# Attention and top-2 mixture of experts on one Trainium2 core: batch 1 routed in halves, scatters and weight parts placed anew, the last batch routed at the first tiles

## Chip, cores and metric

One core of one Trainium2 chip. The metric is the device time of one execution in microseconds (us), the median of the runs; lower is better.

## What is computed

```python
x = L0_attn_x                                   # (4, 1024, 128)
h = layernorm(x)
s = einsum('nsd,ntd->nst', h * w_lhs, h * w_rhs)
x = x + einsum('nst,ntd->nsd', softmax(s), h)
h2 = layernorm(x).reshape(4096, 128)
p = softmax(h2 @ router_w.T)                    # 8 experts, the best two kept and renormalised
y = sum over the two: gate * (gelu(h2 @ w_fc[e] + b_fc[e]) @ w_proj[e] + b_proj[e])
out = x + y
```

## The kernel before, in words

The program is written out by hand for each engine; an engine runs its list in order, and semaphores (`wait_ge`, `then_inc`) tie the lists together. There are two halves: attention over four batches, then the experts in tiles.

**Attention.** A batch b (0 to 3) has 1024 tokens, eight token tiles of 128, in two halves ("units" u = 2b and 2b+1). In stage b TensorE (PE) computes 16 blocks of scores (`score`, L1075 to L1077, three matmuls each, since the operands are split into a high and a low part). VectorE (DVE) takes the maximum of each block (`row_max`, L1409), `join_max` (L1419 to L1425) collects eight of them, PE turns them (`turn_negs`, L1084), ScalarE (ACT) keeps them (`keep_rows`), PE adds them to the scores (`shift_scores`, L1088), ACT takes the exponentials (`exponent`, L922) and PE multiplies with the values (`attend`, L1099, four matmuls a block, eight blocks a half). `add_attention` (L1433 to L1440) divides by the sums and adds to the residual `res`; the last exponentials of a batch wait for `shift_again` (L1414). At the boundary between stages PE also computes the router's sums (`route`, L1111 and L1112), which `keep_hrw` (L1368) reads.

**Routing.** In stage b+1 the logits of batch b are complete (`add_logits`); `take_stats2` and `take_moments2` on DVE and `scale_ln2` on GpSimd (POOL; a power, L740) give the second layernorm, ACT writes the normalised rows (`make_h2`, `high_h2`) and `split_h2` (L1472) their low part. `picks` (12 small DVE instructions) finds the two experts of a token, `rank_round` on PE with `keep_ranks` and `find_slots` on DVE the row of a slot table in DRAM, `gate_powers` on POOL (L783) the gate. Then POOL scatters the rows, 16 indirect DMAs a batch (`dispatch`, L774). A routing "round" is a batch or a half of one: `ROUNDS` lists them, and before the change only batch 2 is in halves. The scatters are paced in POOL's list by waits for a given maximum or exponential (`PACE_OWN`, `PACE_MAX`, `PACE_NEXT`).

**Weights.** ACT scales the eight 128x512 pieces of `w_fc` and POOL subtracts to get their low part (`low_part`, L748): three in the first part of stage 1, two in its second, then `clear_empty` and `store_empty` (L754 to L764) write filler rows into the slot table, which must have landed before the first scatter; the last three come in stage 3.

**Tiles.** 39 tiles of 256 rows, each of one expert. `make_table` (28 small DVE instructions, last L534) says for a group of tiles which expert each has and from which row it is loaded; there are three groups: tiles 0 to 7, 8 to 15, the rest. SyncE (SP) loads a tile (`slots_in`) once the group's table is made and its batches are scattered: batches 0 and 1 for the first group, batch 2 for the second, batch 3 for the third. Step k on PE turns tile k+2 (`turn_slots`, L1269), multiplies tile k up (L1281 to L1283) and tile k-2 down (L1302). ACT does gelu, and in its first steps the second layernorm of batch 3. DVE does `keep_rows` (L1731 to L1739), the bias (`add_bias`, L1746) and the gate (L1753) of tile k-3, and among the first steps the routing of batch 3 and the second table. POOL returns each tile with two indirect DMAs (L873). At the end SP loads all results, DVE adds them and SP stores.

## Time and profile before

| | |
|---|---|
| median of 3 runs | 331.57 us (331.29 to 331.64) |
| the profiled execution | 331.83 us, of which the span is 330.1 us |
| mean granted clock of TensorE | 0.948 of full |
| PE busy | 280.7 us, 85% |
| DVE busy | 225.1 us, 68% |
| ACT busy | 192.6 us, 58% |
| POOL busy | 185.5 us, 56% |
| chain that ended last | PE 59%, DVE 21%, DMA 6%, issue 5%, POOL 4% |

The span counts from the first to the last instruction of the profile; all positions below are us from its start. Stage 1 runs from about 46 to 83, stage 2 to 121, stage 3 to 165, the tiles to 299, and the rest is the way out. A busy share says little here, since each stage has its own limit; idle time of PE and what ended it says more.

### The profile page before, as it was taken

The page shows a single profiled execution, that of the slowest core. Times are in us where ns is not written, and L with a number is a line of the kernel's source. Part 1 is how long each engine was busy: PE and PEld are TensorE (multiplying, and loading weights), DVE is VectorE, ACT ScalarE, POOL GpSimd, SP SyncE. Part 2 cuts the span into 40 slices and gives each one's busy share as a digit, 9 for nine tenths or more (in the row PEclk, how much of TensorE's full clock was granted, in tenths as well). Part 3 has the DMA queues.
Part 4 walks back from the last instruction along what each step waited for, and adds up shares of the span by engine and source line. Part 5 has one row for each costly group of instructions (what it writes and reads, how often), then busy time and mean ns, then how long its engine had stood idle before and what let it go on. Part 6 is the DMA issues. An engine that isn't in the chain of part 4 may idle for free.

```text
span 330.1 us, 7870 instructions
## 1 busy us (share of the span) xinstructions
PE 280.7 (85%) x2197; PEld 250.0 (76%) x2198; DVE 225.1 (68%) x894; ACT 192.6 (58%) x388; POOL 185.5 (56%) x247
## 2 busy tenths in 40 slices
PE   8999998989979995995979999899999999994000
PEld 3588995878858894784968999799999999993000
DVE  4898879898867789799689778345444545453065
ACT  3455567957195634754389877567676767670000
POOL 8030035380777526768778777777777755567200
PEclk9999999999999999799899999999999999998555
DMA  6940000030011100101511531343333321111398
GB/s 204 426 203 0 0 3 0 3 118 13 18 42 43 34 14 29 50 26 42 156 45 44 131 109 52 93 135 101 99 91 88 91 81 47 50 42 48 116 354 317
DMA packets 16948, 29.37 MB, mean 89 GB/s; under 512 B 3760, under 2 KB 12848, under 8 KB 16656
## 3 DMA queue, kind: packets, MB, share of 16 engines
q1 hardware_dynamic: 12080, 18.40, 17.5%
q0 software_dynamic: 4832, 10.53, 9.6%
q8 instruction: 17, 0.28, 0.4%
q14 instruction: 19, 0.16, 0.2%
HBM read 16.30 MB, written 12.62 MB: 88 GB/s over the span
## 4 chain that ended last, share of the span: by engine, by line
PE 59%; DVE 21%; DMA 6%; issue 5%; POOL 4%; ACT 2%; SPq 1%; POOLq 0%; DVEq 0%; ACTq 0%
PE av_ps L1302 17%; PE av_ps L1099 14%; DVE neg_piece L1409 6%; PE sc_ps L1281 4%; PE sc_ps L1282 4%; PE sc_ps L1283 4%; DMA raw_proj<-results 4%; PE bank L1269 2%; PE bank L1088 2%; PE sc_ps L1088 1%; PE bank L1075 1%; DVE tile_start L534 1%; PE bank L1077 1%; PE bank L1076 1%; PE sc_ps L1076 1%
## 5 line engine op out<-in xcount | busy, mean ns | idle before, releaser
L873 POOL DMA_INDIRECT results<-prob,result_row x78 | 74.8, 959 | 32.0 <-issue 12.8
L774 POOL DMA_INDIRECT slots<-stage,slot x64 | 63.6, 993 | 39.1 <-DVE stage L1569 18.8
L1099 PE MATMUL av_ps<-h_all,prob 128*128 128x137 f32 x512 | 73.9, 289 | 3.6 <-DVE lg_part L1440 3.6
L1016 ACT ACTIVATE raw_fc<-sc_ps,bfc,scale_down 128x256 f32<-128x256 f32 x156 | 75.1, 570 | 2.1 <-PE sc_ps L1283 2.1
L1302 PE MATMUL av_ps<-raw_proj,raw_fc 128*128 x624 | 75.8, 275 | 0.0
L1099 PEld LDWEIGHTS av_ps<-h_all,prob 128*128 128x128 f32 x512 | 68.1, 194 | 7.4 <-DVE res L1437 5.1
L1302 PEld LDWEIGHTS av_ps<-raw_proj,raw_fc 128*128 128x128 f32 x624 | 72.6, 192 | 0.5
L1746 DVE TENSOR_TENSOR h_all<-av_ps,bpr 128x256 f32<-128x256 f32 x39 | 16.5, 424 | 48.9 <-PE sc_ps L1283 46.5
L1281 PE MATMUL sc_ps<-h_all,wfc_hi 128*128 128x256 f16 x156 | 42.6, 273 | 1.3 <-ACT raw_fc L1016 1.1
L1008 ACT ACTIVATE h_all<-bank 128x512 f16<-128x512 f16 x39 | 23.2, 596 | 34.5 <-PE sc_ps L1283 30.7
L1282 PE MATMUL sc_ps<-h_all,wfc_hi 128*128 128x256 f16 x156 | 42.5, 273 | 0.0
L1283 PE MATMUL sc_ps<-h_all,wfc_lo 128*128 128x256 f16 x156 | 42.5, 273 | 0.0
L1409 DVE TENSOR_REDUCE neg_piece<-bank 128x1 f32<-128x512 f32 x32 | 21.9, 684 | 8.3 <-PE bank L1077 4.2
L922 ACT ACTIVATE prob<-sc_ps 128x512 f32<-128x512 f32 x32 | 18.4, 599 | 11.4 <-PE sc_ps L1088 11.4
L912 ACT ACTIVATE again<-bank 128x512 f32<-128x512 f32 x16 | 9.5, 593 | 23.5 <-DVE neg_piece L1409 23.5
L1409 DVE TENSOR_REDUCE neg_piece<-sc_ps 128x1 f32<-128x512 f32 x32 | 21.8, 683 | 0.8 <-PE sc_ps L1077 0.7
L1753 DVE TENSOR_SCALAR prob<-h_all,row_gate 128x128 f32<-128x128 f32 x78 | 20.7, 338 | 1.4
L1281 PEld LDWEIGHTS sc_ps<-h_all,wfc_hi 128*128 x156 | 15.2, 98 | 3.6 <-issue 1.8
L932 ACT ACTIVATE h<-res,shift,rstd 128x128 f32<-128x128 f32 x32 | 14.7, 490 | 4.0 <-POOL shift L743 3.3
L1269 PE MATMUL bank<-ident,slots_in 128*128 128x128 f16 x156 | 14.9, 219 | 2.0 <-DMA slots_in<-slots 1.3
L1283 PEld LDWEIGHTS sc_ps<-h_all,wfc_lo 128*128 x156 | 15.3, 98 | 1.8
L1075 PE MATMUL bank<-hT_hi,q_hi 128*128 128x512 f32 x32 | 14.9, 465 | 2.0 <-ACT again L912 1.7
(183 smaller groups left out, 508.4 us busy)
## 6 DMA issues: line engine op xcount, KB each, us to landing
slots_in<-slots SPq DMA_DIRECT2D x39, 132.0 KB, 2.2
raw_fc<-in_w_fc_dram SPq DMA_DIRECT2D x1, 2048.0 KB, 10.9
raw_proj<-in_w_proj_dram SPq DMA_DIRECT2D x1, 2048.0 KB, 15.2
raw_fc<-results SPq DMA_DIRECT2D x2, 1024.0 KB, 7.4
raw_proj<-results SPq DMA_DIRECT2D x2, 1024.0 KB, 12.0
out_dram<-res SPq DMA_DIRECT2D x4, 512.0 KB, 5.0
res<-in_x_dram SPq DMA_DIRECT2D x3, 512.0 KB, 5.8
results<-prob,result_row POOLq DMA_INDIRECT x78, 2.3
```

The lines of the kernel that those rows point to most:

```text
L774: pool.indirect_dma_start(out=slots[:, :], out_offset=bass.IndirectOffsetOnAxis(ap=slot[:, n, k:k + 1], axis=0), in_=stage[:, b % 2, t, :] ...
L873: pool.indirect_dma_start(out=results[:, :], out_offset=bass.IndirectOffsetOnAxis(ap=result_row[a][:, h:h + 1], axis=0), in_=gated[a][h], ...
L1008: act.activation(xT[:, a % NH, :], bank[a % 2][:, :].bitcast(F16)[:, 0:2 * W], ACT.Copy).then_inc(xT_made, 1)
L1016: ins = act.activation(hid[:, a % NH, c, :], up_ps(a, c), ACT.Gelu_apprx_tanh, bias=bfc[:, e, c:c + 1], scale=scale_down[:, 0:1])
L1099: mm = pe.matmul(att[:, t, 0:AUG], probT[:, m % RING, t * P:(t + 1) * P], h_aug[:, b % 2, exp_rows(n), :], start=(n % BT == 0 and t % 2 == ...
L1269: mm = pe.transpose(o[:, part * W + h * P:part * W + (h + 1) * P], x, ident16[:, :])
L1281: pe.matmul(o, wfc_hi[:, e, w], xT[:, a % NH, 0:W], start=True, stop=False, skip_group_check=True)
L1282: pe.matmul(o, wfc_hi[:, e, w], xT[:, a % NH, W:2 * W], start=False, stop=False, skip_group_check=True)
L1283: mm = pe.matmul(o, wfc_lo[:, e, w], xT[:, a % NH, 0:W], start=False, stop=True, skip_group_check=True)
L1302: mm = pe.matmul(o, hid[:, a % NH, c, s], wpr[:, e, c, :], start=(c == 0 and h == 0), stop=(c == HC - 1), skip_group_check=True)
L1409: dve.tensor_reduce(neg_piece[:, r // TU, r % TU, c:c + 1], block_bank(n), AX_X, ALU.max, negate=True).then_inc(max_made, 1)
L1753: ins = dve.tensor_scalar(gated[k % NR][h], biased[:, a % NH, h, :], row_gate[:, a, h:h + 1], None, ALU.mult)
```

## The change

- `ROUNDS`: batch 1 is routed in halves too, so there are 6 rounds instead of 5. Stage 2 gets the code that only stage 3 had: picks among the maxima, an own `rank_round`, an own `find_slots`.
- POOL's list is written out. The low weight parts stand elsewhere: two before the first `scale_ln2`; two, with the filler rows, behind a wait for the sums of the first half of batch 1; the last three behind a wait for those of batch 3 (`beside_sums`). `split_h2` of units 2 and 3 moves from DVE to POOL.
- Scatters: batch 1 has its first eight in stage 2, batch 2 its first four in stage 3, batch 3 its two groups of eight at steps 4 and 6 of the tiles (6 and 7 before).
- DVE takes the first maximum of the next batch, the logits and the statistics before `keep_hrw`. The steps of the first table are spread otherwise. All four `shift_again` of batch 3 stand together, ahead of `find_slots`.
- Batch 3: its picks come ahead of the tiles, its ranks at step 1, its slots at step 2 (steps 1 to 3 and 5 before), and the second table's last steps at 3 and 4.

```diff
-        ROUNDS = [(... if b == B - 2 else (b * BT, (b + 1) * BT)
-                  for b in range(B) for half in range(2 if b == B - 2 else 1)]
+        IN_HALVES = (1, 2)
+        ROUNDS = [(... if b in IN_HALVES else (b * BT, (b + 1) * BT)
+                  for b in range(B) for half in range(2 if b in IN_HALVES else 1)]
...
+            def beside_sums(u):
+                pool.wait_ge(inv_made, u + 1)
...
+            def split_h2(u):
+                b = u // 2
+                pool.wait_ge(h2hi_made, u + 1)
+                part = stage[:, b % 2, (u % 2) * TU:(u % 2 + 1) * TU, :].bitcast(F16)
+                pool.tensor_tensor(part[:, :, D:2 * D], h2[:, :, :], part[:, :, 0:D], ALU.subtract).then_inc(h2lo_made, 1)
...
+            gate_powers(0)
+            beside_sums(2)
+            for i in range(3, EMPTY_PIECES):
+                low_part(i)
+            clear_empty()
+            for half in range(2):
+                store_empty(half)
+            dispatch_beside_exps(0, 0, 1, (11, 12))
...
+            dispatch_beside_maxima(0, 5, 2, (0, 2, 4))
+            gate_powers(1)
+            dispatch_beside_exps(0, 8, 2, (0,))
+            split_h2(2)
+            dispatch_beside_exps(0, 9, 2, (1, 2, 3))
+            scale_ln2(3)
+            dispatch_beside_exps(0, 12, 2, (4, 5, 6, 7))
+            split_h2(3)
+            dispatch_beside_exps(1, 0, 2, (8, 9))
+            gate_powers(2)
+            dispatch_beside_exps(1, 2, 2, range(10, 16))
...
+            dispatch_beside_exps(2, 0, 3, range(4, 8))
+            gate_powers(4)
+            beside_sums(2 * B - 2)
+            for i in range(EMPTY_PIECES, PIECES):
+                low_part(i)
+            for i in range(4, 8):
+                dispatch(2, i)
...
-            LAST_SCATTERS = {6: range(0, 8), 7: range(8, SCATTERS)}
+            LAST_SCATTERS = {4: range(0, 8), 6: range(8, SCATTERS)}
...
+                if isinstance(k, int) and k == 1:
+                    pe.wait_ge(res_made, 2 * B)
+                    pe.wait_ge(lgpart_made, 2 * B)
+                    rank_round(len(ROUNDS) - 1)
...
-                    if b == B - 1 and 1 <= n < 5:
+                    if b >= 2 and 1 <= n < 5:
                         if n == 1:
                             early = picks(ROUNDS_BY[b - 1] - 2)
                         steps(early, (2, 3, 3, 5)[n - 1])
...
-                    split_h2(2 * b - 2)
+                    if b != 2:
+                        split_h2(2 * b - 2)
...
+                    row_max(b + 1, 0)
+                    add_logits(2 * b)
+                    take_stats2(2 * b)
                     keep_hrw(b + 1)
...
-            choose = picks(last)
+            steps(picks(last), 2 * K * E)
+            take_stats2(2 * B - 1)
+            take_moments2(2 * B - 1)
...
-                if k == 5:
-                    keep_ranks(last)
-                    find_slots(last)
+                if k == 1:
+                    find_gap(last)
+                    keep_ranks(last)
+                if k == 2:
+                    find_slots(last)
+                    split_h2(2 * B - 2)
```

How the instructions stand, at three places. **POOL in stage 2**, from the scatters behind `scale_ln2(2)` to the gates of round 2 (`slots<-stage,slot` is a scatter, `neg_mean` the first of the three instructions of `scale_ln2`); before:

```order
L774 DMA slots<-stage,slot 32768x132 x10
L734 TENSOR_SCALAR neg_mean<-moments 128x4
L740 TENSOR_TENSOR rstd<-var,minus_half 128x4
L743 TENSOR_TENSOR shift<-neg_mean,rstd 128x4
L774 DMA slots<-stage,slot 32768x132 x4
L783 TENSOR_TENSOR gate<-euler,gap 128x8
L774 DMA slots<-stage,slot 32768x132 x2
```

and now:

```order
L779 DMA slots<-stage,slot 32768x132 x6
L788 TENSOR_TENSOR gate<-euler,gap 128x4
L779 DMA slots<-stage,slot 32768x132
L795 TENSOR_TENSOR stage<-h,stage 128x4x128
L779 DMA slots<-stage,slot 32768x132 x3
L735 TENSOR_SCALAR neg_mean<-moments 128x4
L741 TENSOR_TENSOR rstd<-var,minus_half 128x4
L744 TENSOR_TENSOR shift<-neg_mean,rstd 128x4
L779 DMA slots<-stage,slot 32768x132 x4
L795 TENSOR_TENSOR stage<-h,stage 128x4x128
L779 DMA slots<-stage,slot 32768x132 x2
L788 TENSOR_TENSOR gate<-euler,gap 128x4
```

Between one `scale_ln2` and the next stand, besides the same ten scatters, a power and a split; before the gates of the next round stand a split and two scatters more.

**POOL in stage 3**, around the last three weight parts (`wfc_lo`), with the semaphores that each waits for; before:

```order
L774 DMA slots<-stage,slot 32768x132 [waits meta_made,h2lo_made,exp_made] x4
L783 TENSOR_TENSOR gate<-euler,gap 128x4 [waits slots_made,gap_made]
L748 TENSOR_TENSOR wfc_lo<-raw_fc,wfc_hi 128x512 [waits w_scaled] x3
L774 DMA slots<-stage,slot 32768x132 [waits meta_made,h2lo_made] x5
L734 TENSOR_SCALAR neg_mean<-moments 128x4 [waits ln2_moments]
```

and now:

```order
L779 DMA slots<-stage,slot 32768x132 [waits meta_made,h2lo_made,exp_made] x4
L788 TENSOR_TENSOR gate<-euler,gap 128x4 [waits slots_made,gap_made]
L749 TENSOR_TENSOR wfc_lo<-raw_fc,wfc_hi 128x512 [waits w_scaled,inv_made]
L749 TENSOR_TENSOR wfc_lo<-raw_fc,wfc_hi 128x512 [waits w_scaled] x2
L779 DMA slots<-stage,slot 32768x132 [waits meta_made,h2lo_made] x6
L735 TENSOR_SCALAR neg_mean<-moments 128x4 [waits ln2_moments]
```

The first of the three waits for `inv_made`, the reciprocals of `add_attention(6)`, and six scatters instead of five stand ahead of `scale_ln2(6)`.

**DVE at the tiles**, the end of the second table (`tile_start` is its last instruction; `row_gate` and `result_row` belong to `keep_rows`, `h_all<-av_ps,bpr` is the bias and `prob<-h_all` the gate of a tile); before:

```order
L528 TENSOR_TENSOR used<-used,capped 128x8 [waits dve_chain]
L531 TENSOR_TENSOR used<-used,capped 128x8 [waits dve_chain]
L534 SCALAR_TENSOR_TENSOR tile_start<-of_expert,tile_last 128x8 [waits dve_chain]
L1731 SCALAR_TENSOR_TENSOR gate_parts<-slots_in,of_expert 128x2 [waits xs_in4]
L1733 SCALAR_TENSOR_TENSOR gate_parts<-slots_in,of_expert 128x2
L1735 SCALAR_TENSOR_TENSOR chosen_row<-slots_in,of_expert 128x2
L1738 TENSOR_TENSOR row_gate<-gate_parts 128x2 [waits row_parts]
```

and now:

```order
L514 TENSOR_TENSOR digits<-of_expert,digit 128x8 [waits dve_chain]
L1739 SCALAR_TENSOR_TENSOR gate_parts<-slots_in,of_expert 128x2 [waits xs_in4]
...
L1746 TENSOR_TENSOR row_gate<-gate_parts 128x2 [waits row_parts]
L1747 TENSOR_TENSOR result_row<-chosen_row,spare_row 128x2
...
L1754 TENSOR_TENSOR h_all<-av_ps,bpr 128x256
L1761 TENSOR_SCALAR prob<-h_all,row_gate 128x128 [waits biased_made]
L1761 TENSOR_SCALAR prob<-h_all,row_gate 128x128
L518 TENSOR_REDUCE turn_number<-digits 128x1 [waits dve_chain]
L521 CAST turn_experts<-turn_number 128x1 [waits dve_chain]
L529 TENSOR_TENSOR used<-used,capped 128x8 [waits dve_chain]
L532 TENSOR_TENSOR used<-used,capped 128x8 [waits dve_chain]
L535 SCALAR_TENSOR_TENSOR tile_start<-of_expert,tile_last 128x8 [waits dve_chain]
```

The `keep_rows` of tile 4 and the bias and gate of tile 1 now stand ahead of the table's last five instructions.

## Rows read from the trace of the kernel before

**Rows 1.** Windows, in order: us, then PE, PEld, DVE, ACT, POOL, clock, DMA share, GB/s
```profile
83.00:121.00 38.00, 35.38 (x239) 30.89 (x239) 29.16 (x104) 21.65 (x44) 23.49 (x30) 1.00 0.09 30
...
121.00:165.00 44.00, 36.08 (x224) 31.16 (x223) 37.50 (x149) 21.88 (x40) 32.03 (x37) 0.92 0.20 59
...
155.60:165.20 9.60, 9.59 (x71) 9.58 (x72) 7.08 (x34) 3.94 (x6) 7.27 (x9) 0.82 0.59 156
...
249.00:298.00 49.00, 49.00 (x468) 47.09 (x468) 24.13 (x118) 35.32 (x73) 30.82 (x34) 1.00 0.23 66
```

**Rows 2.** Timeline of PE: start, us, line, shapes, [idle before, releaser]
```profile
54.98 0.63 PE L1084 MATMUL bank<-ident,neg_cols 128*128 128x128 f32 x4 [1.31 <-DVE neg_cols L1425]
...
68.47 0.49 PE L1088 MATMUL bank<-neg_rows,ones_r 128*128 128x512 f32 x1 [0.86 <-DVE neg_piece L1409]
...
115.06 0.63 PE L1059 MATMUL bank<-ident,h_all 128*128 128x128 f32 x4 [0.65 <-DVE q_lo L1361]
...
131.83 0.91 PE L1084 MATMUL bank<-ident,neg_cols 128*128 128x128 f32 x4 [2.16 <-ACT again L912]
...
155.61 1.64 PE L1099 MATMUL av_ps<-h_all,prob 128*128 128x137 f32 x7 [3.62 <-DVE lg_part L1440]
...
184.92 0.39 PE L1269 MATMUL bank<-ident,slots_in 128*128 128x128 f16 x4
...
213.08 0.40 PE L1269 MATMUL bank<-ident,slots_in 128*128 128x128 f16 x4 [1.29 <-DMA slots_in<-slots]
```

**Rows 3.** Timeline of DVE beside the weight parts
```profile
51.58 0.68 DVE L1409 TENSOR_REDUCE neg_piece<-bank 128x1 f32<-128x512 f32 x1
...
64.88 1.16 DVE L1514 TENSOR_TENSOR pick<-pick,first_id 128x64 f32<-128x64 f32 x1
...
150.15 4.01 DVE L534 SCALAR_TENSOR_TENSOR tile_start<-of_expert,tile_last 128x8 int32<-128x8 f32 x1
```

**Rows 4.** Timeline of POOL: weight parts, fillers, first scatter
```profile
64.79 2.42 POOL L748 TENSOR_TENSOR wfc_lo<-raw_fc,wfc_hi 128x512 f16<-128x512 f32 x2
...
69.76 1.84 POOL L764 DMA_DIRECT2D slots<-raw_fc  x2 [0.32 <-POOL raw_fc L756]
...
83.95 1.12 POOL L774 DMA_INDIRECT slots<-stage,slot  x1 [10.65 <-DVE stage L1569]
...
150.76 3.37 POOL L748 TENSOR_TENSOR wfc_lo<-raw_fc,wfc_hi 128x512 f16<-128x512 f32 x3
```

**Rows 5.** Timeline of DVE, reciprocals of unit 2
```profile
73.29 0.18 DVE L1433 RECIPROCAL inv_sum<-av_ps 128x4 f32<-128x4 f32 x1
```

**Rows 6.** DMAs that store the filler rows
```profile
DMA to landing us min/median/max: 3.7/4.0/4.4
```

**Rows 7.** Groups by form on POOL: busy us, mean ns
```profile
L783 POOL TENSOR_TENSOR gate<-euler,gap 128x4 f32<-128x4 f32 x2 | 2.1, 1044 | 0.0
```

**Rows 8.** Timeline of ACT, second layernorm of unit 3
```profile
105.63 0.88 ACT L932 ACTIVATE h<-res,shift,rstd 128x128 f32<-128x128 f32 x2 [1.36 <-POOL shift L743]
```

**Rows 9.** The chain that ended last: attends at both paces
```profile
96.88 0.93 PE av_ps L1099 x8
...
155.61 9.39 PE av_ps L1099 x64
```

**Rows 10.** Timeline of DVE at the start of the tiles
```profile
165.03 0.18 DVE L1433 RECIPROCAL inv_sum<-av_ps 128x4 f32<-128x4 f32 x1 [2.04 <-PE av_ps L1099]
...
179.87 0.17 DVE L534 SCALAR_TENSOR_TENSOR tile_start<-of_expert,tile_last 128x8 int32<-128x8 f32 x1
...
181.67 0.23 DVE L1541 TENSOR_TENSOR rank<-av_ps,next_slot 128x64 f32<-128x64 f32 x1
...
183.69 0.17 DVE L1569 COPY stage<-row_id 128x8 f32<-128x8 f32 x1
```

**Rows 11.** Loads of slots: SP's queue, and landing
```profile
155.23 72.52 SPq L661 DMA_DIRECT2D slots_in<-slots  x26
...
DMA to landing us min/median/max: 2.0/2.2/4.2
```

More of the change, by code:

```diff
@@ L812, in _, with dispatch_beside_exps, dispatch_beside_maxima @@
+            SCATTERS = K * BT
+            def dispatch_beside_exps(b, first, of, exps):
+                for i, n in enumerate(exps):
+                    pool.wait_ge(exp_made, exp_at(of, n))
+                    dispatch(b, first + i)
+            def dispatch_beside_maxima(b, first, of, maxima):
+                for i, n in enumerate(maxima):
+                    pool.wait_ge(max_made, maxed_at(of, n))
+                    dispatch(b, first + i)
             for u in range(4):
                 scale(u)
[L814 to L851 removed]
@@ L853, in _ @@
-            for i in range(5):
-                dispatch(B - 2, i)
-            scale_ln2(2 * B - 2)
-            for i in range(5, 11):
-                dispatch(B - 2, i)
-            scale_ln2(2 * B - 1)
-            for i in range(11, 15):
-                dispatch(B - 2, i)
-            gate_powers(len(ROUNDS) - 1)
-            for i in range(15, SCATTERS):
-                dispatch(B - 2, i)
-            LAST_SCATTERS = {6: range(0, 8), 7: range(8, SCATTERS)}
+            pool.wait_ge(peak_made, 1)
@@ new lines, in _ @@
+            pool.partition_all_reduce(peaks[:, :], peak[:, :], P, RMAX).then_inc(peaks_made, 1)
+            scale(4)
+            scale(5)
+            low_part(0)
+            low_part(1)
+            scale_ln2(0)
+            low_part(2)
+            scale_ln2(1)
+            gate_powers(0)
[6 more added lines that the diff above has]
+            dispatch_beside_exps(0, 0, 1, (11, 12))
@@ new lines, in _ @@
+            scale(6)
+            scale(7)
+            scale_ln2(2)
+            dispatch_beside_exps(0, 2, 1, (13, 14, 15))
+            dispatch_beside_maxima(0, 5, 2, (0, 2, 4))
[8 more added lines that the diff above has]
+            gate_powers(2)
@@ new lines, in _ @@
+            dispatch_beside_exps(1, 2, 2, range(10, 16))
+            dispatch_beside_maxima(1, 8, 3, (0,))
+            scale_ln2(4)
+            dispatch_beside_maxima(1, 9, 3, (2, 4, 6))
+            gate_powers(3)
+            dispatch_beside_exps(1, 12, 3, range(4))
+            scale_ln2(5)
+            dispatch_beside_exps(2, 0, 3, range(4, 8))
[5 more added lines that the diff above has]
+                dispatch(2, i)
@@ L868, in give_back @@
+            for i in range(8, 10):
+                dispatch(2, i)
+            scale_ln2(6)
+            for i in range(10, 13):
+                dispatch(2, i)
+            scale_ln2(7)
+            gate_powers(5)
+            for i in range(13, SCATTERS):
+                dispatch(2, i)
+            LAST_SCATTERS = {4: range(0, 8), 6: range(8, SCATTERS)}
             def give_back(k, a):
@@ L1605, in _ @@
                         steps(early, (2, 3, 3, 5)[n - 1])
-                    if b == B - 1 and n == 5:
+                    if b >= 2 and n == 5:
                         find_gap(ROUNDS_BY[b - 1] - 2)
@@ L1612, in _ @@
                 if b == B - 1:
-                    steps(first_table, 7)
+                    steps(first_table, 10)
                 row_max(b, 8)
@@ L1674, in _ @@
                 add_attention(2 * b)
-                for r in (0, 1):
+                for r in range(TU) if b == B - 1 else (0, 1):
                     shift_again(b, r)
@@ L1678, in _ @@
                     find_slots(ROUNDS_BY[b - 1] - 1)
-                if b == B - 2:
-                    dve.wait_ge(ranks_kept, 2)
-                    steps(first_table, 3)
                 if b + 1 < B:
-                    if b >= 1:
+                    if b == 1:
                         split_h2(2 * b - 1)
                     low_parts(2 * b + 2)
-                if b == B - 2:
-                    steps(first_table, 3)
-                for r in (2, 3):
-                    shift_again(b, r)
-                if b == B - 2:
-                    steps(first_table, 3)
+                if b + 1 < B:
+                    for r in (2, 3):
+                        shift_again(b, r)
                 if b == 0:
@@ L1779, in step @@
                     gate(k - 3, (a - 3) % NB)
+                if 3 <= k < 5:
+                    steps(second_table, (6, 20)[k - 3])
             run_each_tile(expert_loader(dve, expert), step, 3, lambda group: dve.wait_ge(table_made, group + 1))
```

100 lines of the change are left out of this document (16 added, 84 removed).

## The prediction

> **What bounds the kernel now.** I read the windows first [rows 1]: in the tiles PE is busy for 49.00 of 49.00 us, so whatever reaches the tiles earlier is kept to the end. Stages 2 and 3 do the same attention on PE (35.38 and 36.08 us busy), but stage 3 takes 44 us and stage 2 takes 38: the difference is idle time and a lower granted clock, 0.92 on the mean. So I looked in PE's timeline for the idle time that this change can reach, and for what released each piece [rows 2]: 1.31 us in stage 1's first part (the columns of the maxima), 0.86 in its second, 0.65 at stage 2's end, 3.62 before the last attends, 1.29 before the third group's first tile, all ended by DVE or a DMA.
>
> Then DVE beside POOL's weight parts [rows 3, 4]. The last table instruction, an 8-element one, takes 4.01 us at 150.15 while POOL subtracts its three last parts (3.37 us from 150.76); elsewhere the same instruction takes 0.17 [rows 10]. A pick took 1.16 us at 64.88, beside the two parts from 64.79. So an instruction that reads and writes SBUF can be held for a part's length, 3.37 / 3 = 1.12 us, or for all three. A reduction out of PSUM at 51.58 took 0.68, with a part running beside it.
> The held table instruction stands ahead of the sums of the unit before, for which the last attends wait: their 3.62 us of idle time are mostly that hold. After them PE also ran below its clock, 0.82 on the mean in their window [rows 1].
>
> **The change part by part**, as positions against the profiled execution, 331.83 us; the median is 0.26 below it.
>
> *Stage 1, first part:* row maximum, logits and statistics go ahead of a wait of DVE for the router's sums, and the parts no longer stand beside the maxima's cast. At most PE's idle 1.31 goes; I take -1.2. The same move in stage 3 I put at -0.3, between nothing and the 1.31 of its model.
>
> *Stage 1, second part:* two parts leave 64.79, so the held pick, and with it PE's 0.86 at 68.47, goes: -0.86.
>
> *Filler rows:* the two parts now wait for the reciprocals at 73.29 [rows 5]. From the start of the two parts to the filler's DMAs it was 69.76 - 64.79 = 4.97 us [rows 4], so they are issued at 73.47 + 4.97 = 78.4, the second 1.84 / 2 = 0.9 later, and the slowest landing took 4.4 [rows 6]: 83.8. The first scatter started at 83.95; with 1.0 for the signal to be acted on (SP took 1.07 from a table to a load, below) it would be 84.8. Behind it stands the chain of scatters, second layernorms and rows that ACT and PE want: +0.8, bounds nothing and 1.7.
>
> *Batch 1 in halves:* stage 2 gets one more round: a short matmul on PE, and on DVE ranks and slots, whose chain took 183.86 - 181.67 = 2.2 us [rows 10]. DVE is busy 29.16 of 38 us there [rows 1], so most lies beside PE: I take +0.7, bounds 0.4 and 2.2.
>
> *POOL in stage 2:* between two second layernorms stand one more power, 1.04 us [rows 7], and one split; its price on POOL shows nowhere, the nearest row is the weight part, also a 128x512 subtraction with an f16 result, 1.12. Together 2.2. ACT already waited 1.36 for this layernorm [rows 8], so there is no slack towards ACT; but PE is only reached if ACT falls behind its exponentials. Bounds nothing and 2.2; I take +0.9, under half, since PE had next to no idle time behind that wait.
> What DVE saves in return is the split; with table steps spread it also reaches the low parts of the operands sooner, and the 0.65 at 115.06 goes: -0.65.
> These parts together: -1.2 - 0.3 - 0.86 + 0.8 + 0.7 + 0.9 - 0.65 = **-0.6**.
>
> *Last weight parts behind the sums of batch 3:* the table instruction takes 0.17 instead of 4.01. The last attends then start about 3.4 earlier (the 3.62 less a little that is late next: the last exponentials). They ran 64 in 9.39 us, and in stage 2 eight took 0.93 [rows 9]; without the pause the clock should hold, 8 x 0.93 = 7.4, so 1.9 more. Their end comes 5.3 earlier, and the reciprocals of unit 6 at 165.03 - 5.3 = 159.7. The three parts then run beside the multiply-and-adds of the sums, which read PSUM and one SBUF operand; I cost that at nothing, by the row nearest in kind, the reduction out of PSUM that was not held. If that cover is gone, it is the slower rival below.
>
> *The second table is late next.* From these reciprocals to its end it was 180.04 - 165.03 = 15.0 us [rows 10]. Now ranks and slots come before it (2.2), and a tile's rows, bias and gate, for which DVE spent 1.6 in that region; 15.0 + 2.2 + 1.6 = 18.8, so it ends at 178.5. The first table ended at 154.16 and SP began its loads at 155.23, 1.07 later; a load lands in 2.2 [rows 11]. So tile 8 is there at 181.8, where PE turned it at 184.92 [rows 2]: of 5.3 us only **-3.1** is kept. Nearly the same follows from ACT, whose last second layernorm has six scatters ahead on POOL instead of five.
>
> *Third group:* batch 3 gets ranks and slots at steps 1 and 2 and its scatters at steps 4 and 6. They should be landed several us before tile 16 is turned, and the 1.29 of PE's idle time there [rows 2], with 0.2 of issue, goes: **-1.5**; at worst nothing. Whatever follows the last tile stays as it is.
>
> Sum: -0.6 - 3.1 - 1.5 = -5.2; 331.83 - 5.2 = 326.6 for such an execution, and less 0.26 about **326.4** for the median. With costs at their bounds (filler, round and POOL all high: +3.7; all low: -2.0) it lies between 324.4 and 330.1; they will hardly all fall on one side, so its own range is 324.8 to 328.4.
>
> One rule speaks against a part of the change. The Trainium skill ("SBUF — State Buffer", "SBUF: two separate sides") says that VectorE and GpSimd share one pair of SBUF ports as an exclusive lock for a whole instruction, taken by a VectorE operation in a two-port mode or by one with two SBUF inputs against a GpSimd operation that reads SBUF. By that rule the holds above agree with the trace (4.01 and 1.16 us), the sums out of PSUM go free, and the splits moved to POOL would hold a pick each: if both reached PE in full, the sum would be 2.2 higher, 328.6 instead of 326.4.
>
> **The rivals.**
> 1. *Stage 2 becomes what stage 3 was.* It gets stage 3's structure: more small DVE chains, splits on POOL beside picks, scatters between. Each split could hold an SBUF instruction of DVE for 1.12 us, so 2.2, and if PE pauses its clock falls: the same four matmuls took 0.63 us at 54.98 and 0.91 at 131.83, behind 2.16 idle [rows 2]. For: stage 3 took 6 us longer. Against: 3.62 of these were the held table instruction, and DVE has 9 us free in stage 2. Price +3 on the forecast: 329.4.
> 2. *The parts hold the sums too* (the slower side). If a POOL subtraction holds any DVE instruction with an SBUF operand, also one that reads PSUM, then the parts now stand just where DVE is most wanted: +2.3 behind 73.29, +1.2 by a split at stage 2's end, and 3.37 between 159.7 and the table, which then ends at 181.9, the load lands at 185.1, +0.2 instead of -3.1. Sum: 2.3 + 1.2 + 0.2 - 1.5 - 0.65 = +1.55, about 333.1. It decides from the point where a multiply-and-add beside a part takes a part's length. For: the held instructions all have SBUF operands. Against: the unheld reduction.
> 3. *The start of the tiles absorbs all.* Something other than the table (batch 2's scatters, ACT's rows) keeps tile 8 at 184.92, and the third group's load is just as late as before: 331.2, no change.
> 4. *All goes smoothly:* the table is not late, PE keeps the 5.3, and the unknown costs of stage 2 are at their low end: 326.4 - 2.2 - 1.2 = 323.0.
>
> **How the numbers follow.** Forecast 0.64; rival 1 0.17, of which 0.01 falls within 0.2% (about what a measurement can tell from no change) and 0.01 beyond it on the slower side; rival 2 0.09, rival 3 0.04, rival 4 0.06. Faster: 0.64 + 0.15 + 0.06 = 0.85; same 0.04 + 0.01 = 0.05; slower 0.09 + 0.01 = 0.10. The range runs from rival 4 (323.0) to the upper part of rival 1 (330.6); it leaves out rivals 2 and 3, 0.13, and the edges of the others, some 0.07.
>
> **What would show it.** Right: the first table's last instruction at 0.17; three parts directly behind the reciprocals of unit 6 with multiply-and-adds of usual length beside them; the last attends 3 us earlier, at full clock; PE waiting for the loaded tile 8, at about 181.5; no wait at tile 16. Wrong: pauses of PE over 1 us in stage 2 that ACT's or DVE's work ends, with a lower clock behind; a multiply-and-add of over 1 us beside a part or a split; a first scatter later than 85.5.

## The result and the profile after

| | before | after |
|---|---|---|
| median of the runs, same chip | 331.65 us (20 runs) | 329.13 us (20 runs, 327.14 to 334.12) |
| ratio after / before | | 0.9923, 95% interval 0.9903 to 0.9943 |
| the profiled execution | 331.83 us, span 330.1 | 328.58 us, span 326.8 |
| mean granted clock | 0.948 | 0.953 |

So the change is 2.5 us faster, where the forecast said 5.2. The time lies in the forecast's range (323.0 to 330.6), above its likeliest part, and close to the 329.4 of the first rival.

The changed kernel's times spread more than those of the kernel before, and go with the granted clock: the two runs at 0.959 took 327.1 and 327.2 us, the four at 0.942 and 0.943 330.1 to 331.8. The profiled execution (0.953) gains 3.25, and it is taken apart here. PE's timeline after, with the marks that answer to [rows 2] (start, us, line, shapes, idle before and releaser):

```profile
54.03 0.63 PE L1092 MATMUL bank<-ident,neg_cols 128*128 128x128 f32 x4 [0.54 <-ACT again L920]
...
92.04 1.08 PE L1092 MATMUL bank<-ident,neg_cols 128*128 128x128 f32 x4 [3.40 <-DVE neg_cols L1431]
...
103.72 0.49 PE L1096 MATMUL bank<-neg_rows,ones_r 128*128 128x512 f32 x1 [1.51 <-DVE neg_piece L1415]
...
116.67 0.63 PE L1067 MATMUL bank<-ident,h_all 128*128 128x128 f32 x4
...
133.18 0.63 PE L1092 MATMUL bank<-ident,neg_cols 128*128 128x128 f32 x4 [2.37 <-DVE neg_cols L1431]
...
153.34 7.71 PE L1107 MATMUL av_ps<-h_all,prob 128*128 128x137 f32 x64 [0.41 <-DVE lg_part L1446]
...
183.90 0.40 PE L1277 MATMUL bank<-ident,slots_in 128*128 128x128 f16 x4 [1.70 <-DMA slots_in<-slots]
...
210.66 0.39 PE L1277 MATMUL bank<-ident,slots_in 128*128 128x128 f16 x4
```

What stands at the same place, as positions of PE in both traces, and the gain between one mark and the next beside the forecast's for it:

| PE's mark | before | after | stretch | forecast |
|---|---|---|---|---|
| columns of stage 1, first half | 54.98 | 54.03 | -0.95 | -1.2 |
| columns of stage 1, second half | 71.72 | 69.62 | -1.15 | -0.86 |
| last operands turned in stage 1 | 78.04 | 75.97 | +0.03 | 0 |
| last operands turned in stage 2 | 115.06 | 116.67 | **+3.68** | +1.75 |
| columns of stage 3, second half | 149.28 | 150.22 | -0.67 | -0.3 |
| end of the last attends | 164.99 | 161.05 | -4.88 | -5.3 |
| tile 8 turned | 184.92 | 183.90 | **+2.92** | +2.2 |
| tile 16 turned | 213.08 | 210.66 | -1.40 | -1.5 |
| end of the span | 330.1 | 326.8 | -0.88 | 0 |

Where the forecast had a gain or a loss for a stretch, the measured one has its sign. Two are off by more than 0.5 us to the worse: stage 2 by 1.9, the way from the attends to tile 8 by 0.7. The end is 0.9 better.

**Stage 2.** PE came 2.07 us earlier out of stage 1 and stands at the same place at 92 us (92.04, and 92.14 before): its wait there grew from 1.37 to 3.40 us. DVE's timeline of the changed kernel, for this place and three later ones:

```profile
89.83 0.20 DVE L1539 TENSOR_TENSOR gap<-step_down,rstd 128x4 f32<-128x4 f32 x1 [1.19 <-issue]
...
99.58 1.96 DVE L1563 CAST slot<-slot_f 128x8 int32<-128x8 f32 x1
...
151.30 0.17 DVE L535 SCALAR_TENSOR_TENSOR tile_start<-of_expert,tile_last 128x8 int32<-128x8 f32 x1
...
152.01 1.13 DVE L1443 SCALAR_TENSOR_TENSOR res<-av_ps,inv_sum,res 128x128 f32<-128x128 f32 x4
...
153.15 2.47 DVE L1420 TENSOR_TENSOR again<-again,bank 128x512 f32<-128x512 f32 x4
...
180.70 0.17 DVE L535 SCALAR_TENSOR_TENSOR tile_start<-of_expert,tile_last 128x8 int32<-128x8 f32 x1
```

`gap` (L1539) waited 1.19 us at 89.83, for POOL's power of the second layernorm (the trace puts it down to issue, but that power ends at 89.75 and the code waits for it). It stands between the maxima now, so the last two maxima, the columns and PE wait with it. The cast of the slots (L1563) at 99.58 takes 1.96 us. The three rows around 151 to 153 answer to [rows 3]: the table instruction takes 0.17, not 4.01; four multiply-adds of the sums take 1.13 together and four repeated shifts 2.47, all of them out of PSUM, beside the three weight parts. POOL's timeline, where both waits come from:

```profile
76.28 1.85 POOL L769 DMA_DIRECT2D slots<-raw_fc  x2 [0.32 <-POOL raw_fc L761]
...
83.29 1.10 POOL L779 DMA_INDIRECT slots<-stage,slot  x1 [5.17 <-DMA slots<-raw_fc]
...
88.73 1.02 POOL L741 TENSOR_TENSOR rstd<-var,minus_half 128x4 f32<-128x4 f32 x1
...
100.32 1.18 POOL L795 TENSOR_TENSOR stage<-h,stage 128x512 f16<-128x512 f32 x1
...
152.06 3.41 POOL L749 TENSOR_TENSOR wfc_lo<-raw_fc,wfc_hi 128x512 f16<-128x512 f32 x3 [0.35 <-DVE inv_sum L1439]
```

The filler rows go out at 76.28, the first scatter waits for them to land and starts at 83.29, and the power that `gap` needs (88.73) stands behind two scatters and two other layernorms. POOL idled 5.17 us ahead of that scatter. The split on POOL at 100.32 to 101.50 ends when DVE's cast ends (99.58 + 1.96 = 101.54). The cast began 0.74 us before the split by the record, while a scatter was being issued (99.27 to 100.30); the run with the splits on DVE, below, tells the two apart. The second split, at 112.15 to 113.33, stands beside the four multiply-adds of a sum out of PSUM (112.37 to 113.50), and these took their usual 1.13 us: it held nothing. ACT waited for the same layernorm as `gap`:

```profile
90.05 0.88 ACT L940 ACTIVATE h<-res,shift,rstd 128x128 f32<-128x128 f32 x2 [3.37 <-POOL shift L744]
```

**The clock.** Windows of the changed kernel (us, then busy of PE, PEld, DVE, ACT, POOL, granted clock, DMA share, GB/s): the pause at 92, the work behind it, the last attends, the tiles.

```profile
88.00:95.00 7.00, 3.43 (x14) 2.31 (x12) 3.10 (x9) 3.34 (x8) 5.38 (x9) 0.76 0.09 30
...
92.00:98.00 6.00, 5.60 (x24) 4.32 (x25) 3.34 (x10) 4.39 (x11) 4.78 (x5) 0.77 0.18 58
...
153.00:161.20 8.20, 7.86 (x70) 7.87 (x71) 7.64 (x36) 4.78 (x9) 6.81 (x8) 1.00 0.58 145
...
249.00:298.00 49.00, 48.60 (x461) 46.60 (x459) 23.96 (x114) 32.96 (x68) 30.01 (x32) 1.00 0.21 63
```

Around the pause the granted clock is 0.76; the four matmuls at 92.04 took 1.08 us instead of 0.63 to 0.66. In the last attends it is 1.00 where [rows 1] had 0.82, and they took 7.71 us instead of the 9.39 of [rows 9].

### The profile page after: what moved, and what is told of

Its sections match the earlier page's. It is cut to its first block, busy times and chain, and to the rows that moved or that the text cites. A ratio compares the mean times of both kernels' runs of the same rounds, so it can differ in the third digit from the quotient of the medians.

```text
span 326.8 us, 7906 instructions
## 1 busy us (share of the span) xinstructions
PE 278.5 (85%) x2198; PEld 248.1 (76%) x2199; DVE 225.0 (69%) x918; ACT 193.1 (59%) x388; POOL 188.2 (58%) x250
## 4 chain that ended last, share of the span: by engine, by line
PE 56%; DVE 15%; issue 9%; POOL 9%; DMA 7%; ACT 2%; SPq 1%; POOLq 1%; DVEq 0%; ACTq 0%
PE av_ps L1306 18%; PE av_ps L1107 10%; PE sc_ps L1289 5%; DVE neg_piece L1415 5%; PE sc_ps L1290 4%; PE sc_ps L1291 4%; POOL slots L779 4%; DMA raw_proj<-results 4%; PE bank L1277 2%; PE av_ps L1056 2%; DMA slots<-raw_fc 2%; POOL results L881 2%; POOL wfc_lo L749 1%; PE bank L1096 1%; PE sc_ps L1096 1%
## 5 line engine op out<-in xcount | busy, mean ns | idle before, releaser
L1107 PE MATMUL av_ps<-h_all,prob 128*128 128x137 f32 x512 | 72.3, 285 | 0.4 <-DVE lg_part L1446 0.4
L1107 PEld LDWEIGHTS av_ps<-h_all,prob 128*128 128x128 f32 x512 | 66.3, 190 | 4.1 <-DVE res L1443 1.9
L1289 PEld LDWEIGHTS sc_ps<-h_all,wfc_hi 128*128 x156 | 15.2, 98 | 3.6 <-issue 2.1
L1290 PEld LDWEIGHTS sc_ps<-h_all,wfc_hi 128*128 x156 | 15.3, 98 | 1.3
```

Source lines behind the costliest of these rows:

```text
L1107: mm = pe.matmul(att[:, t, 0:AUG], probT[:, m % RING, t * P:(t + 1) * P], h_aug[:, b % 2, exp_rows(n), :], start=(n % BT == 0 and t % 2 == ...
L1289: pe.matmul(o, wfc_hi[:, e, w], xT[:, a % NH, 0:W], start=True, stop=False, skip_group_check=True)
L1290: pe.matmul(o, wfc_hi[:, e, w], xT[:, a % NH, W:2 * W], start=False, stop=False, skip_group_check=True)
```

## The experiments

Eighteen runs follow, on five chips. **A matter of the chip comes first.** On two of the chips the kernel before takes 331.8 us, on three 365 to 369 us. The traces of these three show where the time goes: PE pauses for about a microsecond between matmuls of a tile, with nothing that released it. The same stretch of the tiles on such a chip (the kernel with the gap moved) and in the kernel before:

```profile
185.00:225.00 40.00, 25.37 (x165) 21.09 (x164) 12.74 (x67) 13.92 (x30) 24.36 (x27) 0.74 0.25 72
```

```profile
185.00:225.00 40.00, 38.53 (x368) 36.19 (x367) 24.20 (x121) 28.36 (x59) 30.54 (x32) 1.00 0.38 106
```

25.37 us of PE's work in 40 us, at a mean clock of 0.74, against 38.53 at 1.00. The pauses begin at 99 us, so positions up to there compare with any trace; times don't, and nor do ratios. Three kernels ran on both kinds of chip: with the parts' wait alone, 0.9859 on such a chip and 1.0007 on an ordinary one; with POOL's norms first and no such wait, 0.974 and 1.0021; with the norms first and the gap moved, 0.9718 and 0.9894. Where such a ratio stands below, it is called throttled, and no verdict rests on it.

### Stage 2: the gap, the splits and POOL's order (throttled chip)

Moving the gap:

```diff
-                    if b >= 2 and n == 5:
+                    if b == 3 and n == 5:
                         find_gap(ROUNDS_BY[b - 1] - 2)
                 join_max(2 * b)
+                if b == 2:
+                    find_gap(ROUNDS_BY[b - 1] - 2)
```

> The changed kernel with one step moved: in stage 2 the gap of round 1 (L1539) stands behind the columns of the maxima instead of between the maxima. Theory A (DVE's wait for POOL's second layernorm inside find_gap holds the last two maxima, and PE's pause behind them lowers its clock): PE's pause at 92 us falls from 3.40 to 1.4-2.2 us, the clock stays full, and the time falls by 1.5 to 3 us against the changed kernel. Theory B (what costs in stage 2 is the instructions that a split on GpSimd holds, and DVE's added work): no change within 0.5 us.

Throttled: 0.9855 (0.981 to 0.9899). PE's row, and then ACT's:

```profile
91.51 0.66 PE L1092 MATMUL bank<-ident,neg_cols 128*128 128x128 f32 x4 [2.83 <-ACT again L920]
```

```profile
90.10 0.88 ACT L940 ACTIVATE h<-res,shift,rstd 128x128 f32<-128x128 f32 x2 [3.38 <-POOL shift L744]
```

The wait of PE went from 3.40 to 2.83 only, and its releaser is ACT now, which still waits until 90.1 for the shift of the layernorm. So theory A was half right: the wait is in the chain, but the late layernorm reaches PE by two ways, DVE's gap and ACT's rows.

Splits on DVE (`split_h2(2)` and `split_h2(3)` taken out of POOL's list, DVE's conditions `b != 2` and `b == 1` made to include them):

> The changed kernel with the splits of units 2 and 3 back on DVE. Theory B (the split on GpSimd holds an SBUF-to-SBUF instruction of DVE, the 1.96 us cast of the slots at 99.6 us, and with it a maximum): the cast takes 0.17, PE's wait of 1.51 us at 103.7 goes, DVE pays 0.68 for each split; 0.8 to 1.5 us faster. Theory A: the pause at 92 us stays at 3.4, so most of the lost gain stays lost.

Throttled: 0.9863 (0.9828 to 0.9897). DVE's cast of the slots (L1560 here):

```profile
100.17 0.17 DVE L1560 CAST slot<-slot_f 128x8 int32<-128x8 f32 x1
```

0.17 instead of 1.96, and a scatter was being issued beside this cast too (99.34 to 100.37): with the split gone from POOL the hold is gone, so it was the split and not the scatter. PE's wait behind it was 0.61 instead of 1.51, that at 92 us stayed at 3.42. Both together:

> Both edits together. If stage 2's loss is these two costs and they add: 2.5 to 4.5 us faster than the changed kernel, some 325 to 326.5 us. Rival (the table of the second group, late behind the sums, or the load of tile 8, eats what arrives earlier): the tiles start earlier, PE waits longer than 1.7 us at tile 8, under 1 us is left.

Throttled: 0.9872 (0.983 to 0.9915), 360.86 us beside 360.23 and 360.9 for the two alone. No addition can be read; what it costs or brings in time is not settled here.

POOL's second layernorm of unit 2 ahead of the two first ones:

```diff
+            scale_ln2(2)
             scale(6)
             scale(7)
-            scale_ln2(2)
```

> The changed kernel with the second layernorm of unit 2 ahead of the two first layernorms of batch 3 on POOL; DVE's list untouched. Theory A: its power ends 2.9 us earlier (86.9 instead of 89.8), so the gap no longer waits, and PE's pause at 92 us falls to about 1.4-2.2 us: 1.5 to 3 us faster, like moving the gap. If the position of the gap in DVE's list costs by its own work and not by its wait: no change.

Throttled: 0.983 (0.9796 to 0.9865).

```profile
90.93 1.09 PE L1092 MATMUL bank<-ident,neg_cols 128*128 128x128 f32 x4 [2.29 <-DVE neg_cols L1431]
```

With DVE's list untouched the pause falls to 2.29 and PE stands at 90.93, 1.1 us earlier. So POOL's order sets 1.1 us of the place at 92 us; a pause of 2.29 us is left, and the four matmuls behind it took 1.09 us.

### The order of POOL, on an ordinary chip

Here the changed kernel itself ran again, on the same chip as the three runs behind it.

> The changed kernel itself, on the chip and beside the runs that the experiments share, so that they can be compared with it. If the chip does not matter its ratio to the kernel before is 0.990 to 0.994; if TensorE's lower clock in the tiles on a chip scales everything, the same ratio within 0.003.

Measured 329.81 us (12 runs), ratio 0.9937 (0.9905 to 0.9969), the same as the first time. Beside it:

```diff
-            dispatch_beside_exps(0, 0, 1, (11, 12))
             scale(6)
             scale(7)
             scale_ln2(2)
+            dispatch_beside_exps(0, 0, 1, (11, 12))
```

> The changed kernel with the two first layernorms and the second layernorm of unit 2 ahead of the first two scatters on POOL, where POOL idles 5.2 us for the filler rows to land. Theory A (corrected: DVE's gap and ACT's rows wait for POOL's second layernorm, which stands behind scatters that wait for the filler rows; moving the gap alone left ACT's wait): the power ends at 85 instead of 89.8, ACT's rows start 4 us earlier, PE's pause at 92 us falls from 3.4 to under 1.3, and the time falls 2 to 3.5 us against the changed kernel on the same chip. Rival (PE's lead is lost to DVE's work between the maxima in any case): pause over 2, under 1 us faster.

Measured 327.22 us (6 runs), ratio 0.9895 (0.9851 to 0.9939). POOL, DVE and PE of this run:

```profile
83.99 1.02 POOL L741 TENSOR_TENSOR rstd<-var,minus_half 128x4 f32<-128x4 f32 x1
...
85.97 1.15 POOL L779 DMA_INDIRECT slots<-stage,slot  x1 [0.69 <-issue]
```

```profile
88.62 0.16 DVE L1539 TENSOR_TENSOR gap<-step_down,rstd 128x4 f32<-128x4 f32 x1
...
97.81 1.72 DVE L1571 TENSOR_TENSOR stage<-stage,gate 128x4 f32<-128x4 f32 x1
```

```profile
90.80 0.63 PE L1092 MATMUL bank<-ident,neg_cols 128*128 128x128 f32 x4 [2.21 <-DVE neg_cols L1431]
...
101.28 0.51 PE L1096 MATMUL bank<-neg_rows,ones_r 128*128 128x512 f32 x1 [1.35 <-DVE neg_piece L1415]
...
151.59 7.72 PE L1107 MATMUL av_ps<-h_all,prob 128*128 128x137 f32 x64 [0.41 <-DVE lg_part L1446]
...
182.24 0.40 PE L1277 MATMUL bank<-ident,slots_in 128*128 128x128 f16 x4 [1.68 <-DMA slots_in<-slots]
```

```profile
90.80:96.80 6.00, 5.69 (x35) 4.40 (x36) 3.85 (x14) 4.94 (x12) 4.76 (x6) 1.00 0.18 58
```

The power starts at 83.99 instead of 88.73, the gap takes 0.16 and waits for nothing, and PE's columns are at 90.80, 1.24 us earlier; the marks at the end of stage 2 (114.25 against 116.67) and at tile 8 (182.24 against 183.90) are 2.4 and 1.7 earlier. Half of the 2.4 is the earlier place at 90.80; the other half is the clock, 1.00 in the six microseconds behind the pause where the changed kernel had 0.77. A pause of 2.21 stays: DVE's picks now stand between the maxima, and DVE has no idle time from 84 to 90.5. The rival was half right there. The hold merely moved to another instruction, the 1.72 us at 97.81. The median is 2.6 us lower on the same chip, but the two intervals overlap: the traces show the gain clearly, the times only probably.

> The order of POOL of the run before, with the splits of units 2 and 3 on DVE and the second table finished in step 3. If the three costs of the changed kernel (late layernorm, held cast, late table) add: 3 to 5 us faster than the changed kernel. Rival: the later waits eat the earlier gain, and it is within 1 us of the run before.

Measured 331.56 us (12 runs), ratio 0.9983 (0.9958 to 1.0007): the gain is gone. The second table ended at 178.05, earlier than the 180.87 of the changed kernel, and tile 8 waited for no DMA. But (the two turns are those of tiles 7 and 8):

```profile
179.38 3.41 PE L1303 MATMUL av_ps<-raw_proj,raw_fc 128*128 x16 [2.63 <-DVE h_all L1750]
182.58 0.63 PE L1274 MATMUL bank<-ident,slots_in 128*128 128x128 f16 x4
...
186.24 0.39 PE L1274 MATMUL bank<-ident,slots_in 128*128 128x128 f16 x4
```

PE waited 2.63 us for the bias of tile 0 (`h_all`), which now stood behind the table's last instructions on DVE, and turned tile 8 at 186.24, 4.0 us later than with the norms first alone (182.24). Half of that comes from the tiles: from the turn of tile 6 to that of tile 8 it took 11.2 us instead of 9.2. So by the traces the place that the change gave the table's end, behind a tile's rows, bias and gate, was the better of the two. The other half was lost before the tiles: the last attends started at 153.71 instead of 151.59, and in the stretch ahead of them the granted clock was 0.89 here and 1.00 with the norms first alone:

```profile
135.00:152.00 17.00, 16.66 (x107) 14.59 (x106) 12.71 (x59) 10.48 (x19) 9.80 (x12) 0.89 0.10 33
```

```profile
135.00:152.00 17.00, 16.26 (x112) 14.07 (x112) 14.28 (x65) 11.77 (x23) 11.60 (x14) 1.00 0.12 35
```

Whether the splits on DVE brought that lower clock isn't shown. What they did in stage 2 is: PE's pause at 101 us is 0.35 us here instead of 1.35, and yet the last operands are turned at 114.64 instead of 114.25; the granted clock from 91 to 108.2 us was 0.90 here, against 1.00.

The same table with the gap moved and the splits on DVE, on a throttled chip:

> The changed kernel with the gap moved, the splits on DVE, and the second table finished in step 3, ahead of the rows, bias and gate. Theory (tile 8 is bound by the second table): its load is issued some 1.5 us earlier, PE's wait there goes, 1 to 1.7 us faster than the same kernel without the table's move; about 324 to 325.5. Rival (batch 2's last scatter, or ACT's rows behind POOL's second layernorm, bound tile 8): under 0.4 us.

Throttled: 0.9832 (0.9783 to 0.9882), against 0.9872 for the same kernel with the table late on another throttled chip; not settled by this, and the trace from the ordinary chip speaks against it.

### The parts' wait for the sums

Into the kernel before, one line:

```diff
                 if b == B - 1:
+                    pool.wait_ge(inv_made, 2 * B - 1)
                     for i in range(EMPTY_PIECES, PIECES):
                         low_part(i)
```

> The kernel before with one wait added: the last three weight parts on POOL wait for the reciprocals of batch 3's first sums. Predicted mechanism: the last table instruction takes 0.17 instead of 4.01, the last attends start 3.4 us earlier and run at full clock, their end comes 4 to 5.3 earlier; tile 8 is then bound by the second table or by batch 2's last scatter and the net gain is 2 to 3 us. Rival: the gain is all given back at tile 8: within 0.5 us.

Throttled: 0.9859 (0.9807 to 0.9911). Again, on the ordinary chip:

> The kernel before with only the wait of the last three weight parts, again. If this one wait carries the whole gain, its ratio is that of the changed kernel or better (0.985 to 0.993); if the rest of the change adds to it, the changed kernel is 0.3% or more faster on the same chip.

Measured 331.96 us (12 runs), ratio 1.0007 (0.9989 to 1.0025): alone it brings nothing. PE, DVE and POOL of this run:

```profile
152.57 7.72 PE L1100 MATMUL av_ps<-h_all,prob 128*128 128x137 f32 x64 [0.41 <-DVE lg_part L1441]
...
184.94 0.40 PE L1270 MATMUL bank<-ident,slots_in 128*128 128x128 f16 x4 [3.83 <-DMA slots_in<-slots]
```

```profile
175.90 0.17 DVE L534 SCALAR_TENSOR_TENSOR tile_start<-of_expert,tile_last 128x8 int32<-128x8 f32 x1
```

```profile
151.29 3.40 POOL L748 TENSOR_TENSOR wfc_lo<-raw_fc,wfc_hi 128x512 f16<-128x512 f32 x3 [0.35 <-DVE inv_sum L1434]
...
179.56 1.03 POOL L774 DMA_INDIRECT slots<-stage,slot  x1 [0.19 <-issue]
```

The attends start at 152.57, 3 us earlier than before, at full pace, and the second table ends at 176.07, 4 us earlier. All of it is lost at tile 8: PE waits 3.83 us for its load and turns it at 184.94, where it was at 184.92. The last scatter of batch 2 starts at 179.56, and at 179.58 in the kernel before: POOL works from 151.29 to there almost without a pause, 16 indirect DMAs of that batch at 1.26 us each being most of it. The load of tile 8 needs that batch complete.

Now the same wait taken out of the changed kernel (`beside_sums(2 * B - 2)` left out):

> The changed kernel without the wait of the last three weight parts for the sums. Theory (the wait is what brought the gain of stage 3): an SBUF instruction of DVE beside the parts is held again, the last attends start 2 to 3.5 us later than 153.3, and the whole is 1 to 3 us slower than the changed kernel. Rival (with all repeated shifts together the table is done before the parts start, so the wait is not needed): within 0.5 us.

Throttled: 0.9953 (0.9923 to 0.9983); the kernel with only the gap moved had 0.9855 on another throttled chip. With POOL's norms first, beside a kernel that has the wait (and has the gap behind the columns):

> The run with POOL's norms first, without the wait of the last three weight parts for the sums. Theory: an instruction of DVE beside the parts is held, the sums ahead of the last attends are late, the last attends start 2 to 4 us later; since the load of tile 8 was waited for 1.7 us only, 1 to 3 us slower. Rival: the tiles' start absorbs it: within 0.5 us.

> The run with POOL's norms first, and the gap of round 1 behind the columns of the maxima on DVE as well. With the layernorm early, the gap no longer waits (0.16 us at 88.6), so moving it frees only its own 0.3 us: pause at 91 us 1.9 instead of 2.2, within 0.5 us of the run with the norms first. If it is over 1 us faster, DVE's place of the gap costs more than its wait.

Throttled: 0.974 without the wait, 0.9718 with it (0.9696 to 0.9784 and 0.9681 to 0.9755). On the ordinary chip:

> The run with the norms first but without the wait of the weight parts for the sums, once more, beside the run before. Where the clock holds in the tiles: the last attends end 4 to 5 us later, of which the start of the tiles absorbs a part, so 1 to 3 us slower than with the wait. If all is absorbed: within 0.5 us.

> The run with POOL's norms first and the gap behind the columns, once more. On a chip whose TensorE keeps its clock in the tiles: 326.5 to 327.5 us, within 0.5 us of the run with the norms first alone; on a throttled chip its ratio says little of the changed kernel.

Measured 332.21 us without (12 runs), ratio 1.0021 (0.9989 to 1.0053), and 327.77 with (6 runs), 0.9894 (0.9862 to 0.9926). The two differ in the gap's place too; the norms first alone, which differ by the wait only, had 0.9895. The wait is worth about 4 us by either, more than was expected. The profiled execution without the wait took 335.61 us, 3.4 more than the median of its kernel, so its lines show the mechanism and not the price. DVE and POOL without it, then PE without and with it:

```profile
152.55 4.00 DVE L525 TENSOR_TENSOR used<-capped 128x8 f32<-128x8 f32 x1
```

```profile
153.16 3.37 POOL L749 TENSOR_TENSOR wfc_lo<-raw_fc,wfc_hi 128x512 f16<-128x512 f32 x3
```

```profile
158.21 10.59 PE L1106 MATMUL av_ps<-h_all,prob 128*128 128x137 f32 x64 [3.82 <-DVE lg_part L1445]
```

```profile
151.22 7.71 PE L1107 MATMUL av_ps<-h_all,prob 128*128 128x137 f32 x64 [0.41 <-DVE lg_part L1446]
```

It is the plain copy of the hold in [rows 3]: 4.00 us for an 8-element instruction beside three parts of 3.37 us. The sums are late, PE waits 3.82 and its attends then take 10.59 us instead of 7.71. Of the 7.0 us between the two starts of the attends 3.6 had built up before, by 144 us: the granted clock was 0.83 from 130 to 150 there, against 0.91 with the wait.
As for the gap behind the columns: 0.9894 beside 0.9895 for the norms first alone, no difference, as expected (PE's columns at 90.56 instead of 90.80).

The last of this family, the splits on DVE with the norms first:

> The run with POOL's norms first, with the splits of units 2 and 3 on DVE. Theory (a split on GpSimd holds one small SBUF instruction of DVE, 1.72 us at 97.8, and PE pauses 1.35 us behind it): the pause at 101 us falls to about 0.3 and the run is about 1 us faster. Rival (what fills DVE, 0.68 us a split, costs as much later, in front of the operands of the next batch): within 0.5 us.

Throttled: 0.975 (0.9704 to 0.9796), beside 0.9718; no gain from it can be shown.

### The last batch's routing

The change's last part alone in the kernel before (picks ahead of the tiles, ranks at step 1, slots at step 2, scatters at 4 and 6):

> The kernel before with the last batch's routing and scatters as in the change (picks ahead of the tiles, ranks at step 1, slots at step 2, scatters at steps 4 and 6). Predicted: the 1.3 us pause at tile 16 goes, 1.0 to 1.5 faster. Rival: the routing ahead of the second table makes tile 8 late, so the pause moves there: no gain, or slower by up to 3 us, since the table's end (180.0 before) moves by up to 3.8.

Throttled: 1.0019 (0.9985 to 1.0054). And with the parts' wait:

> The kernel before with the wait of the weight parts for the sums and the last batch's routing and scatters as in the change, but without batch 1 in halves. Theory (the whole list of scatters behind the parts sets when batch 2 is complete; only the halves of batch 1, which let four scatters of batch 2 go in stage 3, free it): tile 8 is turned at 184.9 as before, the pause at tile 16 goes, 1.0 to 1.5 us faster than before. Rival (the table or the start of the tiles decides, not the scatters): tile 8 at 183 or earlier, 2.5 us or more faster than before.

Throttled: 0.999 (0.9956 to 1.0024). Neither is faster than the kernel before. Every kernel with batch 1 in halves and the parts' wait had 0.987 or lower on such chips, but so had the parts' wait alone, without the halves (0.9859). So these ratios do not show a backlog of scatters, and what the last batch's routing costs or brings by itself is open.

## Why the prediction came out as it did

**Right.** Stage 1: -2.1 forecast, -2.07 measured. The hold of the table instruction and its price came as forecast: the instruction took 0.17, the attends ran at full clock, and 4.88 of the 5.3 us were gained. The sums out of PSUM are not held beside the parts (1.13 us for four), so the slower rival falls. The pause at tile 16: -1.40 of -1.5. One wrong reading did no harm: the reciprocals at 165.03, called those of unit 6, are those of unit 7. Unit 6's, which release the parts, come ahead of the last attends (151.79 after), so the parts ran beside that sum and its shifts.

**The term that was mis-sized: stage 2, +1.75 forecast, +3.68 measured.** Inside it two steps failed.
- *Filler rows, +0.8.* The scatter's start was put at 84.8, worked out from the reciprocals at their old place; it came at 83.29, 0.66 earlier than before. But PE arrived 2.07 earlier, and the chain that it waits for, fillers, two scatters, three layernorms, did not move with it. The sum counted stage 1's lead in full and the chain's delay by the positions of the old trace; the lead of an engine counts only up to the slowest chain that it waits for, and that gained 0.66. The gap's place was a part of this that no step had: "batch 1 in halves" was costed by DVE's work (+0.7), while the new code also put a wait for POOL, 1.19 us, ahead of two maxima. The norms ahead of the scatters give 2.4 of stage 2's 3.68 back, which is this step's share with the clock that the pause cost. What stays of the pause, 2.21 us against 1.37 before, is DVE's picks between the maxima, 0.84 us, about what "batch 1 in halves" was costed at (+0.7).
- *POOL in stage 2, +0.9.* It counted the time the split takes on POOL, not what it holds on DVE. The first split held a 0.17 us cast for 1.96 us, with a pause of PE of 1.51 us behind it; the second held nothing. The first rival had the hold, at 1.12 for each of the two, and its 329.4 is near the measured time; its mechanism was half of what came, since it did not have the late layernorm, and that the price fits is in part luck. How much of the 3.68 the hold is stays open: without it the pause went (0.35 us), but the end of stage 2 came no earlier. By the Trainium skill's rule ("SBUF — State Buffer", "SBUF: two separate sides"), under which a split on GpSimd can hold a VectorE instruction, the sum would have been 2.2 higher, 328.6, which is nearer than the forecast. The run with the split taken off POOL agrees that the split was the holder (0.17 us).

**Between the attends and tile 8** the forecast had +2.2 and +2.92 came. The table decided, as forecast: it ended at 180.87 instead of 178.5, 1.4 of it because the attends ended later than 159.7 and 1.0 because it took 19.8 us from the reciprocals instead of 18.8. That the table alone decided was luck: in the kernel before, with the wait alone, batch 2's scatters did, and all was lost. The forecast put the gain down to the wait; the runs show that the wait alone stands at 1.0007 and the rest of the change without it at 1.0021 (with the norms first). Both are needed. By the trace of the wait alone, what the rest adds at tile 8 is the scatters moved ahead, though no run moves them by themselves: in the change four of batch 2's sixteen go out in stage 3, and its last one started at 175.21 instead of 179.58.

**What stays open**: the price of the splits' place in time, which on an ordinary chip was tried only together with the early table; and the last batch's routing by itself, which ran on throttled chips only. Of the 0.88 us after tile 16, which no term named, 0.44 had come by the last tile (the tiles just behind tile 16 stood further apart before) and 0.44 came behind it, in the way out; why is open.

## To carry to other kernels

When an engine is made faster in one stage, follow it to the next wait and ask which chain releases it there: its lead counts only as far as that chain moved too. Of an added instruction count the wait inside it and what is queued behind it, and, on GpSimd, what it holds on VectorE (here 1.96 us of a 0.17 us cast). Two bounds in parallel (here a table and a queue of scatters) show no gain until both are moved.

## What the hardware showed beside this

- A small SBUF-to-SBUF instruction of DVE beside a GpSimd subtraction took 1.72 and 1.96 us beside one of 1.18 us, and 4.00 us beside three in a row of 3.37 us together: it was held over all three, not for one. In each of these cases it had started 0.5 to 0.8 us before the recorded start of the subtraction. Where it started after it, in [rows 3], the pick at 64.88 was held for one part only (1.16 us, with two parts in a row beside it), and the next instruction (L1518, at 66.08) for the second (1.22 us). The reciprocals, multiply-adds and shifts that read PSUM ran beside the same three at full pace.
- Chips differ. On three of five chips PE was paused in the tiles and the kernel before took 10 to 11% longer, and the ratio of one kernel to it moved by up to 2.8% between such a chip and an ordinary one (0.974 and 1.0021).
- A pause of PE can cost twice, but its length alone doesn't say whether. After 3.40 us the next four matmuls took 1.08 us instead of 0.63. After 2.2 us at the same place they took 0.63 with the norms first, and 0.86 with the early table; without the parts' wait they took 0.63 in one execution and 0.90 in another of the same kernel. With the gap moved they took 0.66 after 2.83 us, and with the one layernorm first 1.09 after 2.29. The spread of the times with their granted clock may come from this; that isn't shown.
